# One wait on the exponentials for both heads of a score step, and one for the four products of a values group

## The reference

```
qkv = einsum('bchw,oc->bohw', x, w_qkv);  q, k, v = split(qkv, 3, axis=1)
q = q.reshape(b, 8, 64, n) * 64**-0.5;  k, v = the same shape
attn = softmax(einsum('bhdi,bhdj->bhij', q, k), axis=-1)
out = einsum('bhij,bhdj->bhid', attn, v)          # back to b, 512, 32, 32
y = einsum('bchw,oc->bohw', out, w_out) + b_out
y = y * rsqrt(mean(y * y, over channels) + 64**-0.5) * rms_scale
return y + x
```

## Time and profile before

| | |
|---|---|
| median of 3 runs | 4412.9 us (4409.09 to 4414.07) |
| the profiled execution's own time | 4412.16 us |
| its span, first to last instruction | 4410.4 us |
| TensorE busy (matmul) | 4146.6 us, 94% |
| VectorE, GpSimd, ScalarE busy | 65%, 64%, 51% |
| mean granted TensorE clock | 0.975 |

### The profile page before, as it was taken

The page is one execution under the profiler, slowest core; times in us unless marked ns, Lnnn a source line. Parts: engine busy times, 40 slices in busy tenths (PEclk is TensorE's granted clock), DMA queues, the critical chain, the costliest instruction groups (busy, mean ns, idle before and its releaser), DMA issues.

```text
span 4410.4 us, 53031 instructions
## 1 busy us (share of the span) xinstructions
PE 4146.6 (94%) x18624; PEld 2434.4 (55%) x18624; DVE 2866.3 (65%) x2700; ACT 2266.8 (51%) x3969; POOL 2837.1 (64%) x2188
## 2 busy tenths in 40 slices
PE   7999999999999999999999999999999999999996
PEld 5555555555555555555555655555555555555553
DVE  4666666666666666666676766666666666666665
ACT  3555455455555555454554545545555455454553
POOL 4566666666666656666666666667666666666666
PEclk8999999999999999999999999999999999999998
DMA  3111111111111111111011010110111111111110
GB/s 135 39 48 39 48 39 61 45 48 39 58 48 39 48 39 58 48 39 67 29 53 53 32 65 29 58 49 34 62 44 43 48 39 58 48 39 48 39 39 29
DMA packets 71270, 212.19 MB, mean 48 GB/s; under 512 B 8152, under 2 KB 8280, under 8 KB 58208
## 3 DMA queue, kind: packets, MB, share of 16 engines
q1 hardware_dynamic: 71008, 208.80, 13.3%
HBM read 168.92 MB, written 39.85 MB: 47 GB/s over the span
## 4 chain that ended last, share of the span: by engine, by line
PE 57%; issue 20%; POOL 13%; ACT 7%; DVE 3%; DMA 0%; POOLq 0%; ACTq 0%; SPq 0%; DVEq 0%
PE aux L442 12%; PE pv L587 12%; PE score L572 8%; POOL prob_sum L975 8%; PE aux L475 7%; PE score L574 6%; PE aux L499 5%; PE aux L553 5%; ACT probs L656 2%; POOL prob_sum L971 2%; POOL resid L988 1%; DVE rms_b L869 1%; PE aux L507 1%; POOL x_lo L285 1%; ACT q_hm L665 1%
## 5 line engine op out<-in xcount | busy, mean ns | idle before, releaser
L975 POOL TENSOR_TENSOR prob_sum<-prob_sum,probs 128x512 f32<-128x512 f32 x1536 | 1984.5, 1315 | 672.1 <-ACT probs L656 669.8
L831 DVE TENSOR_REDUCE maxima<-aux 128x1 fp32r<-128x1024 f32 x1024 | 1206.1, 1219 | 998.6 <-PE aux L553 928.3
L656 ACT ACTIVATE probs<-score 128x512 f32<-128x512 f32 x2048 | 1112.0, 594 | 990.5 <-PE score L574 982.9
L587 PE MATMUL pv<-probs,v_sb 128*64 128x512 f32 x4096 | 1005.6, 612 | 0.0
L572 PE MATMUL score<-q_hl,k_hh 128*128 128x512 f32 x2048 | 895.5, 437 | 8.2 <-ACT probs L656 6.4
L574 PE MATMUL score<-q_hm,k_l 72*128 72x512 f32 x2048 | 823.7, 402 | 0.0
L971 POOL TENSOR_TENSOR prob_sum<-probs 128x512 f32<-128x512 f32 x256 | 339.5, 1347 | 657.0 <-ACT probs L656 657.0
L442 PE MATMUL aux<-x_hi,w_ring 128*128 128x512 f32 x2048 | 668.6, 408 | 19.7 <-POOL x_lo L285 11.2
L572 PEld LDWEIGHTS score<-q_hl,k_hh 128*128 128x128 f32 x2048 | 392.8, 192 | 281.4 <-issue 178.9
L587 PEld LDWEIGHTS pv<-probs,v_sb 128*64 128x64 f32 x4096 | 251.9, 138 | 495.7 <-issue 428.7
L442 PEld LDWEIGHTS aux<-x_hi,w_ring 128*128 128x128 f32 x2048 | 359.2, 189 | 175.5 <-issue 66.4
(11 more groups left out here) (74 smaller groups left out, 4447.2 us busy)
## 6 DMA issues: line engine op xcount, KB each, us to landing
w_ring<-w_split SPq DMA_DIRECT2D x93, 1024.0 KB, 4.8
x_stage<-x SPq DMA_DIRECT2D x128, 256.0 KB, 4.1
resid<-x SPq DMA_DIRECT2D x128, 256.0 KB, 5.7
out<-resid SPq DMA_DIRECT2D x128, 256.0 KB, 2.0
w_split<-w_ring SPq DMA_DIRECT2D x3, 1024.0 KB, 12.0
w_split<-y_sb SPq DMA_DIRECT2D x3, 1024.0 KB, 3.8
y_sb<-wqkv SPq DMA_DIRECT2D x4, 512.0 KB, 8.7
probs<-wqkv SPq DMA_DIRECT2D x2, 512.0 KB, 7.8
```

The lines of the kernel that those rows point to most:

```text
L587: pe.matmul(pv[half][e * D:(e + 1) * D, :], v_sb[:, pair // 2, j, (pair % 2) * P + e * D:(pair % 2) * P + (e + 1) * D], probs[:, j % 4, e, ...
L656: act.activation(probs[:, j % 4, e, :], score[e][:], ACT.Exp, scale=SOFT).then_inc(prob_ready, 1)
L831: dve.tensor_reduce(maxima[:, n:n + 1], bank(k, 2), AX_X, ALU.max).then_inc(aux_free[k], 1)
L975: pool.tensor_tensor(prob_sum[:, e, :], prob_sum[:, e, :], probs[:, j % 4, e, :], ALU.add).then_inc(prob_added, 1)
```

## The change

The scores of a step wait once, before head 0, for the exponentials of both heads of the step before. The products of values wait once for a pair of steps, for all four exponentials of it. The order of the matmuls is the same.

```diff
             def scores(body, slot, j):
                 pair, half = divmod(slot, 2)
+                n = body.b * 128 + slot * 16 + 2 * j
+                if not (body.first and slot == 0 and j == 0):
+                    pe.wait_ge(prob_ready, n)
                 for e in range(2):
-                    n = body.b * 128 + slot * 16 + 2 * j + e
-                    if not (body.first and slot == 0 and j == 0):
-                        pe.wait_ge(prob_ready, n - 1)
                     if j == 0 and e == 0:
                         pe.wait_ge(mask_ready, body.b * SLOTS + slot + 1)
...
                 b = body.b - 1 if back else body.b
+                if j % 2 == 0:
+                    pe.wait_ge(prob_ready, b * 128 + slot * 16 + 2 * j + 4)
                 for e in range(2):
-                    n = b * 128 + slot * 16 + 2 * j + e
-                    pe.wait_ge(prob_ready, n + 1)
                     if j == 0 and e == 0 and not (body.first and slot == 0):
                         pe.wait_ge(sums_copied, b * SLOTS + slot)
```

## The result

The changed kernel takes 4441.5 us (median of 6 runs, 4438.28 to 4442.59) against 4413.0 for the one before (6 runs): ratio 1.0065, 95% interval 1.0052 to 1.0078. It is 28.5 us slower. The prediction said slower, 4422 us, within 4412 to 4430: the direction was right, the size was wrong by a factor of three.

A forecast was written before the change was run, and what follows sets the result against it. TensorE's own order was taken as the bound. Seven even batches (7.0 to 7.4 us) and the last batch (2.0) added 9.0 to 9.4 us to 4412.16, giving 4421.5; with 0.7 for the median 4422, range 4412 to 4430.

The forecast's parts named there:

- The removed waits are worth nothing: 1024 score waits and 1536 value waits removed on TensorE's loads: 0 us, at most 5 us.
- Late steps: 54 of 1023 steps where head 0's score load comes before the second exponential has ended: direct sum +5.4 us.
- The three places: Slot 5 step 2, slot 2 step 3 and slot 2 step 7, where the stricter score wait binds in nearly every batch.
- the covers: Later TensorE waits in slot 5 and slot 2 hide the delays of steps 2 and 3: cost 0, uncovered 7.8 and 3.0 us.
- Slot 5's wait for x_lo: TensorE's idle time after slot 5 step 2, forecast to shrink from 2.8 to 2.3 us.
- slot 2's for the maxima: TensorE's idle time after slot 2 step 3, forecast to shrink from 2.45 to 2.26 us.
- The even batch draws slot 5's low clock: V projection in even batches moves from 117.7 to 118.2 us after slot 1's low stretch and draws half clock: +1.5 us.
- This 2.0 us of delay: Even batch's slot 2 and slot 5 delay, half returned at next slot 1: 1.0 us left per even batch.
- Slot 2 step 7, "+0.48, in full": Head 0's load in even batches moves from 2321.77 to 2322.25, uncovered: 7 x 0.48 = 3.4 us; odd batches +0.02.
- The sum: 1.0 us per even batch, 7.0 to 7.4 us for seven, plus 2.0 in the last batch: 9.0 to 9.4 us.
- Rival (2): Every batch draws all its low clock stretches and slot 1 returns nothing: 15.9 us, 4429; chance 0.13.
- Rival (3): Shorter idle times draw no low clock in slot 5, odd batches too: about 0, without give-back 4406; chance 0.10.

The follow-up runs named there:

- kernel with all late steps but one: The whole change except in slot 2 step 7, where scores wait per head as in the kernel before: 4414.5 us, 1.0006.
- filled kernels: Kernel before and changed kernel, each with matmuls of constants in TensorE's idle times of slots 1, 2 and 5: 4365.7 us (0.9896) and 4388.9 us (0.9949).
- unfilled kernels: Without added matmuls: the changed kernel (4441.5 us), and the kernel before with only the scores' part (4441.1) or only slot 2 step 7 merged (4436.2).
- filled changed one: Changed kernel with 24, 9 and 8 matmuls of constants in the idle times of slots 1, 2 and 5: 4388.9 us, 0.9949.
- filled kernel before: Kernel before with 24, 9 and 8 matmuls of constants in the idle times of slots 1, 2 and 5: 4365.7 us, 0.9896.
- same delay made with work: Two matmuls of constants (0.46 us) ahead of slot 2 step 7's scores, in the kernel before (4422.3 us, 1.0024) and the changed kernel (4428.4, 1.0036).

## Why the prediction was right in direction and wrong in size

- *The removed waits are worth nothing.* Right: 1.0003 for the values alone. The 127 instructions that went belong to the scores' part (the kernel with the values' part alone has none fewer). They stood at most before head 1 of a slot's first scores, and head 1's load comes 0.46 us behind head 0's there, before and after.
- *Late steps.* The three places and the covers were right. Slot 5's wait for x_lo shrank from 2.77 to 2.3 us, slot 2's for the maxima from 2.45 to 2.42. I had forecast 2.26 for the second: the late load did move by 0.18 us, but the idle time before the load of the projection that follows step 3 took it up (0.39 us before, 0.20 after). The kernel with all late steps but one is 2.8 us slower; its trace shows 0.3 of it in batches 1 to 14 and 1.3 in the last. Step 7 of slot 2 was right by kind of batch and not by number: in the shorter kind the load moved by 0.48, in the longer kind by 0.3 with nothing left of it (15.64 before, 15.63 after). That even batches show 0.43, close to the 0.48 forecast for them, is luck: it is the difference between the two kinds.
- *The even batch draws slot 5's low clock.* Right for the shorter kind of batch, and the reason given holds: in all 14 batches instead of 7, +1.41 us against 1.5. The 118.2 us worked out for it lie on the side of 117.96 on which every batch draws it.
- *"This 2.0 us of delay is partly given back at the next slot 1 ... half of each delay returns."* This step failed. Over a pair slot 1 costs what it did: the +0.50 of batch 7 and the -0.48 of batch 8 are the two kinds changing places. The 1.0 us that I took off for each pair, 7 us in all, did not come back.
- *Slot 2 step 7, "+0.48, in full".* This step failed too, and is the larger part: the term left out the clock, and it measured 2.02 over steps 5 to 7 in the batch that pays it, 0.48 of delay and some 1.5 of a low stretch. I had compared the times of the loads there but not asked what the clock makes of the added idle time, which I asked for slot 5 only. This kind of batch has no low clock at step 5, so its step 7 waits for ScalarE's copy (0.38 and 0.66 us), and the stricter wait comes on top of that.
- *The sum.* Per pair of batches: slot 1 0.0, slot 2 2.0, slot 5 1.4, together 3.4 where I had 1.0. Seven pairs make 23.6. For the last batch I had 2.0 us and it shows 4.5: it was of the longer kind before and is of the shorter kind now, which by batches 7 gives 1.58 more in slot 2 and 0.5 in slot 1, beside its late steps.
- *The range.* Rival (2), the clock falling more often and nothing given back, was the nearest, and its 4429 was short by the seven low stretches of slot 2 (10 us), a place that was not in it, and by 2.5 us in the last batch.
- *Rival (3), faster by shorter idle times,* fell: slot 5's idle is shorter and draws the low clock more often. The Trainium skill (TensorE: Matmul & The Clock Gate, "Why this matters for your kernels") advises against idle gaps between bursts of matmuls beyond a certain length; of the gaps here only slot 1's, of about 6 us, is that long. The filled kernels agree with it (0.9896), and slot 1's gap draws the low clock in every batch. But gaps of 2.3 us did so as well and gaps of 2.8 us did not always, so the length of a single gap did not decide here, and the measurement stands.

In short, the loads, covers and the change in slot 5 came out, and two terms failed: the half given back at slot 1 was nothing, and step 7 of slot 2 cost 2.02 us in each pair and not 0.48, because its added idle time draws a low clock stretch.

What stays open: why the lengths of the batches settle where they do. The start of a projection after slot 1's low stretch tells whether a stretch follows at slot 5 and at slot 2 step 5, but no run shows what places slot 1's own stretch, or why 9 of 14 equal batches draw one at step 7 in the filled kernel.

## What to carry to other kernels

A wait that is merged with a later one costs nothing where the waiting engine arrives late anyway; look through the trace for the few steps in which it doesn't, here 3 places in 64, and ask of each what idle time already stands next to it. Compare batches of one kind before and after: a change can make two kinds change places, and a comparison by number then mixes them up. On TensorE, price added idle time by the clock as well as by its length: 0.49 us of wait cost 24 us in all at a place with two short idle times beside it, and under 3 us in all where it lay inside a longer wait of TensorE. Where a tuned kernel leaves TensorE idle for a few us in every iteration, matmuls of constants in the gap can be worth more than the tuning of waits: filled, the kernel before is 1.0% faster, and that version beats both kernels of this study.

## What the runs showed of the hardware

- A low clock stretch can follow several short idle times. At slot 2 step 7 the matmul rows show 0.38, 0.66 and 0.47 us of idle, and the clock stood at 0.50 from 2062.2; 19 of 19 such batches had it in the unfilled kernels, 9 of 14 in the filled changed one. With the first two idle times alone the kernel before had 1.00 there (0 of 7 batches), the filled kernel before a stretch in 2 of 14.
- The same delay made with work drew no stretch at that place (0 of 9 batches).
- Equal idle times draw the low clock or not by when they fall. Slot 5's, 2.26 to 2.80 us, drew it in each of 117 batches in which it ended 117.96 us or more after slot 1's low stretch, and in none of 23 in which it ended by 117.89.
- 0.46 us of plain work more per batch cost 0.97 us per batch (14.5 us in 15 batches); five more low stretches behind slot 5's idle account for most of the excess.
- Satisfied waits on a weight load left no mark: with 2559 fewer waits in the program and 127 fewer instructions the loads of scores keep their pace of 0.23 us, and with the 1536 of the values alone the ratio is 1.0003.
